# First attention layer by key/value group, its value and score products in high and low parts, four heads side by side

## The chip, the cores and the metric

The kernel runs on one core of one Trainium2 chip. A core has a tensor engine for matrix products (PE, with its weight loads shown apart as PEld), VectorE (DVE), ScalarE (ACT), GpSimd (POOL) and SyncE (SP), which here only issues transfers. Each engine works through its own list of instructions in order; semaphores join the lists. SBUF is the working memory, PSUM holds the results of products in eight banks of 512 fp32 columns. The metric is the device time of one launch in microseconds (us), lower is better.

## The reference, cut to what matters

Four layers follow each other, each with an attention part and a feed-forward part that read the same normalized input and are added to the stream `x` of 2 x 1024 tokens of width 256. Only the first layer's attention is touched. It has 16 query heads of width 128 in 4 groups; the 4 heads of a group share one key head and one value head. (The lines below leave out a multiplication and division by a layer index of 1; the drawn shapes are those that the kernel runs, 2 batches of 1024 tokens.)

```python
xn = _layernorm(x, axis=-1)
q = jnp.einsum('bsh,he->bse', x, w_q).reshape(b, sq, GROUPS, HPG, KVC)
kv = jnp.einsum('bsh,he->bse', x, w_kv)
k, v = jnp.split(kv, 2, axis=-1)
...
scores = jnp.einsum('bqgpd,bkgd->bgqpk', q, k) * (SCALE / LAYER_INDEX)
...
scores = jnp.where(causal[None, None, :, None, :], scores, -jnp.inf)
probs = jax.nn.softmax(scores, axis=-1).astype(x.dtype)
ctx = jnp.einsum('bgqpk,bkgd->bqgpd', probs, v).reshape(b, sq, HEADS * KVC)
return jnp.einsum('bse,eh->bsh', ctx, w_dense)
```

## The kernel before

Everything is kept turned, features on the 128 partitions and tokens along the free side. `XT` is the stream, `XN` the normalized stream, and `XH`, `XL` are `XN` split in two: a high part rounded to the type float32r and the low part that the rounding left. `split_product` (line 199) makes one precise product of three float32r ones (high with high, high with low, low with high), for each of the two halves of the width of 256; the projections use it. The other products of this attention (scores, values, dense) are plain fp32; the profile records two instructions for one of these.

`l0_attn` calls two stages. `l0_kv` loads the whole key/value weight, splits it, and projects all keys `KT` and values `V` in 32 jobs of 512 columns over eight banks. `l0_heads` then loops over the 16 heads. Its unit u is one tile of 128 queries: U = 16 units a head, 8 in each batch, and tile t of a batch sees t+1 blocks of 128 keys. One head is a software pipeline, written out in its order in each engine's loop body, over steps s:

- PE: `scores(s)` into one of two score banks of 1024 columns (line 355), then `turn_probs(s-2)`, which transposes the blocks of probabilities (369), `dense(s-4)` (391), and `weigh_values(s-3)` with 128 columns at a time (382). The queries of the next head are projected in the last steps, into the score banks.
- DVE: `invert(s-1)` (459), `row_max(s)` with causal mask, maximum and its negative (450 to 454), `keep_turned(s-2)` for every second group of up to four turned blocks (470), `add_dense(s-4)` into `XT` (475).
- ACT: `keep_ctxT(s-4)` (521), `keep_turned(s-2)` for the other groups (514), `exp(s)` with its row sum (528), and the copies of the queries (497).
- POOL multiplies the probabilities by the inverse of the sum (424) and makes the low part of the query weight (413).

SP loads each head's query and dense weights ahead of their use. What holds a score bank is the chain of scores, mask, maximum, negative, exp; four buffers of probabilities follow it. The wait of ACT's turned copy is only for PE:

```python
act.wait_ge(turned, h * G + n + 1)
if u >= 2:
    act.wait_ge(pv_done, h * U + u - 1)
```

Of the kernel before, what the change touches and what calls it, by code (L numbers as in the profile page):

```python
# [16 lines left out]
P = 128  # L17
# [191 lines left out]
def l0_attn(nc, k, a):  # L209
    with Stage(nc, "l0a") as st:  # L210
        KT = st.sb("KT", [P, L0_GROUPS, T])
        V = st.sb("V", [P, TT, L0_GROUPS * L0_HD])
        l0_kv(nc, k, a, KT, V)
        l0_heads(nc, k, a, KT, V)


def l0_kv(nc, k, a, KT, V):

    with Stage(nc, "l0kv") as st:
        acc = [st.ps(f"acc{i}") for i in range(8)]  # L220
        w_loaded, made, kept_act, kept_dve = st.sem("w_loaded"), st.sem("made"), st.sem("kept_act"), st.sem("kept_dve")
        GD = L0_GROUPS * L0_HD
        wkv = st.sb("wkv", [P, DC, 2 * GD])
        w_hi, w_lo = st.sb("w_hi", [P, DC, 2 * GD], F32R), st.sb("w_lo", [P, DC, 2 * GD], F32R)
        whi_ready, wlo_ready = st.sem("whi_ready"), st.sem("wlo_ready")

        jobs = [("k", g, j) for g in range(L0_GROUPS) for j in range(NJ)] + [("v", t, 0) for t in range(TT)]

        def target(n):
            kind, i, j = jobs[n]  # L230
            return KT[:, i, j * BANK:(j + 1) * BANK] if kind == "k" else V[:, i, :]

        with nc.Block() as block:

            @block.sync
            def _(sp):
                sp.dma_start(wkv[:, :, :], rows(a["L0_attn_w_kv"])).then_inc(w_loaded, 16)

            @block.tensor
            def _(pe):  # L240
                pe.wait_ge(wlo_ready, DC)
                for n, (kind, i, j) in enumerate(jobs):
                    if n >= 8:
                        pe.wait_ge(kept_act if n % 2 == 0 else kept_dve, (n - 8) // 2 + 1)
                    if kind == "k":
                        tok, col = slice(j * BANK, (j + 1) * BANK), slice(i * P, (i + 1) * P)
                        mm = split_product(pe, acc[n % 8][:, :], lambda c: w_hi[:, c, col], lambda c: w_lo[:, c, col],
                                           lambda c: k.XH[:, c, tok], lambda c: k.XL[:, c, tok])
                    else:
                        tok, col = slice(i * P, (i + 1) * P), slice(GD, 2 * GD)  # L250
                        mm = split_product(pe, acc[n % 8][:, :], lambda c: k.XH[:, c, tok], lambda c: k.XL[:, c, tok],
                                           lambda c: w_hi[:, c, col], lambda c: w_lo[:, c, col])
                    mm.then_inc(made, 1)

            @block.scalar
            def _(act):
                act.wait_ge(w_loaded, 16)
                for c in range(DC):
                    act.activation(w_hi[:, c, :], wkv[:, c, :], ACT.Copy).then_inc(whi_ready, 1)
                for n in range(0, len(jobs), 2):  # L260
                    act.wait_ge(made, n + 1)
                    act.activation(target(n), acc[n % 8][:, :], ACT.Copy).then_inc(kept_act, 1)

            @block.vector
            def _(dve):
                for c in range(DC):
                    dve.wait_ge(whi_ready, c + 1)
                    dve.tensor_tensor(w_lo[:, c, :], wkv[:, c, :], w_hi[:, c, :].bitcast(F32), ALU.subtract).then_inc(wlo_ready, 1)
                for n in range(1, len(jobs), 2):
                    dve.wait_ge(made, n + 1)  # L270
                    dve.tensor_copy(target(n), acc[n % 8][:, :]).then_inc(kept_dve, 1)


def l0_heads(nc, k, a, KT, V):


    U = B * NQ
    GPB = sum(-(-(t + 1) // 4) for t in range(NQ))
    G = B * GPB
    group_of = [(u, g) for u in range(U) for g in range(-(-(u % NQ + 1) // 4))]  # L280
    first_group = [group_of.index((u, 0)) for u in range(U)]

    with Stage(nc, "l0h") as st:
        wq = st.sb("wq", [P, DC, P])
        wq_hi, wq_lo = st.sb("wq_hi", [P, DC, P], F32R), st.sb("wq_lo", [P, DC, P], F32R)
        whi_ready, wlo_ready = st.sem("whi_ready"), st.sem("wlo_ready")
        wd = st.sb("wd", [P, D])
        QT = st.sb("QT", [P, T])
        probs = st.sb("probs", [P, 4, S])
        VG = st.sb("VG", [P, TT, P])  # L290
        PT = st.sb("PT", [P, 2, NQ, P])
        ctxT = st.sb("ctxT", [P, 2, P])
        top = st.sb("top", [P, 2])
        negtop = st.sb("negtop", [P, 2])
        total = st.sb("total", [P, 4])
        inv = st.sb("inv", [P, 4])
        sc = [st.ps(f"sc{i}", 2 * BANK) for i in range(2)]
        tp = [st.ps(f"tp{i}") for i in range(2)]
        cx = st.ps("cx")
        outp = st.ps("outp")  # L300
# [2478 lines left out]
```

## Time and profile before

| | |
|---|---|
| median of 3 runs | 3993.09 us (3988.18 to 3993.31) |
| the profiled execution's own time | 3988.51 us |
| its span, first to last instruction | 3986.7 us |
| mean granted clock of PE over the span | 0.932 |
| busy share of the span | PE 89%, PEld 66%, DVE 59%, ACT 39%, POOL 35% |

A share over the whole span mixes four layers. The changed stages are the first quarter of the span, and what they are bound by is read there. "Idle before" in a group of instructions is the time in which its engine stood before them, with what ended it. A record of a product includes the tail in which the array empties, which overlaps the next product; the distance between starts is what a product takes in a row of them.

### The profile page before, as it was taken

How to read it: one execution, taken by the hardware profiler on the slowest of the kernel's cores; microseconds unless marked ns; L12 is line 12 of the kernel's file. 1: busy time of each engine (PE TensorE's matmuls, PEld its weight loads, DVE VectorE, ACT ScalarE, POOL GpSimd, SP SyncE). 2: the span in 40 equal slices, each digit the busy share in tenths (PEclk: the TensorE clock that was granted, in tenths of full speed). 3: DMA queues.
4: the chain of work that ended last, by engine and by line, in shares of the span. 5: the costliest groups of instructions: out<-in, count | busy, mean ns of one | idle time of the engine just before them, and what ended most of it. 6: DMA issues, size and time to landing. Idle time of an engine off the chain costs nothing. (4 is left out here: it accounts for less than half of the span.)

```text
span 3986.7 us, 65977 instructions
## 1 busy us (share of the span) xinstructions
PE 3548.5 (89%) x21608; PEld 2615.5 (66%) x21608; DVE 2353.9 (59%) x4783; ACT 1557.1 (39%) x2820; POOL 1383.1 (35%) x1085
## 2 busy tenths in 40 slices
PE   6899999999797999999986599999699997999576
PEld 4777777777575888888862344444388856886354
DVE  3555555655423656666655677775477746776444
ACT  2444444444333444444432246664233333333111
POOL 1333333333133666666643200000133352335144
PEclk8999999999898999999998889999799998999755
DMA  0000000000001000000002311221233303331144
GB/s 33 7 5 3 5 5 5 3 5 5 32 0 43 18 18 17 17 17 17 17 0 74 121 74 75 76 75 40 64 93 105 98 15 101 93 104 49 58 107 96
DMA packets 115990, 178.66 MB, mean 45 GB/s; under 512 B 22288, under 2 KB 65040, under 8 KB 115600
## 3 DMA queue, kind: packets, MB, share of 16 engines
q1 hardware_dynamic: 109776, 169.38, 13.8%
q0 software_dynamic: 6144, 8.39, 1.3%
q8 instruction: 38, 0.62, 0.1%
q14 instruction: 32, 0.26, 0.0%
HBM read 151.51 MB, written 25.95 MB: 45 GB/s over the span
## 5 line engine op out<-in xcount | busy, mean ns | idle before, releaser
L424 POOL TENSOR_TENSOR l0h_probs<-l0h_probs,l0h_inv 128x128 f32<-128x128 f32 (+7 forms) x256 | 292.8, 1146 | 585.7 <-DVE l0h_inv L459 585.7
L1747 DVE TENSOR_REDUCE l2h_half<-l2h_s 128x1 f32<-128x512 f32 x512 | 329.5, 685 | 94.9 <-PE l2h_s L1658 94.9
L1734 ACT ACTIVATE l2h_PT<-l2h_s 128x1024 f32<-128x1024 f32 x256 | 261.9, 1023 | 194.9 <-PE l2h_s L1668 194.6
L355 PE MATMUL l0h_sc<-l0a_KT,l0h_QT 128*128 x768 | 296.8, 499 | 30.0 <-ACT l0h_probs L528 28.4
L382 PE MATMUL l0h_cx<-l0h_PT,l0h_VG 128*128 128x128 f32 x2304 | 300.7, 276 | 0.0
L528 ACT ACTIVATE l0h_probs<-l0h_sc,l0h_negtop 128x128 f32<-128x128 f32 (+7 forms) x256 | 189.7, 741 | 245.3 <-DVE l0h_negtop L454 244.9
L382 PEld LDWEIGHTS l0h_cx<-l0h_PT,l0h_VG 128*128 128x128 f32 x2304 | 278.0, 192 | 1.0
L159 POOL TENSOR_TENSOR XN<-XN,n_rstd 128x512 f32<-128x512 f32 x32 | 39.9, 1266 | 633.6 <-DVE n_rstd L140 633.6
L1658 PE MATMUL l2h_s<-l2h_K,l2h_Q 128*128 128x512 f32 x512 | 180.1, 428 | 22.5 <-DMA l2h_K<-l_split 18.8
L452 DVE TENSOR_REDUCE l0h_top<-l0h_sc 128x1 f32<-128x128 f32 (+7 forms) x256 | 194.0, 758 | 8.8
L355 PEld LDWEIGHTS l0h_sc<-l0a_KT,l0h_QT 128*128 128x128 f32 x768 | 125.6, 192 | 106.6 <-issue 63.7
L1668 PE MATMUL l2h_s<-l2h_Q,l2h_K 128*128 128x512 f32 x512 | 187.2, 447 | 1.0 <-DMA l2h_Q<-l2h_mlo 0.6
L391 PE MATMUL l0h_outp<-l0h_ctxT,l0h_wd 128*128 128x128 f32 x1024 | 163.8, 283 | 24.9 <-ACT l0h_ctxT L521 11.7
L369 PEld LDWEIGHTS l0h_tp<-ident,l0h_probs 128*128 128x128 f32 x1152 | 138.5, 141 | 64.2 <-issue 39.6
L369 PE MATMUL l0h_tp<-ident,l0h_probs 128*128 128x128 f32 x1152 | 168.7, 274 | 0.0
L470 DVE COPY l0h_PT<-l0h_tp 128x256 f32<-128x256 f32 (+2 forms) x192 | 98.6, 514 | 114.2 <-PE l0h_tp L369 112.3
L2158 POOL TENSOR_TENSOR l3p_w_lo<-l3p_w,l3p_w_hi 128x1024 fp32r<-128x1024 f32 x34 | 80.1, 2356 | 241.4 <-ACT l3p_w_hi L2114 241.4
L391 PEld LDWEIGHTS l0h_outp<-l0h_ctxT,l0h_wd 128*128 128x128 f32 x1024 | 134.2, 191 | 44.7 <-ACT l0h_ctxT L521 31.2
L514 ACT ACTIVATE l0h_PT<-l0h_tp 128x512 f32<-128x512 f32 (+1 forms) x192 | 100.8, 525 | 159.7 <-PE l0h_tp L369 159.2
L2190 DVE TENSOR_TENSOR_SCAN l3p_table<-l3p_decb,l3p_eye 128x512 f32<-128x512 f32 x128 | 149.6, 1210 | 23.0 <-DMA l3p_blk<-c_l_block 17.4
L1680 PE MATMUL l2h_pv<-l2h_PT,l2h_VH 128*32 128x256 f32 x2048 | 162.1, 391 | 0.2 <-ACT l2h_ctxT L1725 0.2
L2148 POOL TENSOR_TENSOR l3a_Y<-l3p_skip,l3p_sz 128x512 f32 (+1 forms) x64 | 81.7, 1276 | 209.3 <-DVE l3p_skip L2181 209.3
(408 smaller groups left out, 8869.8 us busy)
## 6 DMA issues: line engine op xcount, KB each, us to landing
l3p_decb<-l_decays SPq DMA_DIRECT2D x128, 256.0 KB, 4.2
l3p_w<-L_w SPq DMA_DIRECT2D x34, 512.0 KB, 3.7
l2h_Q<-l_split SPq DMA_DIRECT2D x64, 256.0 KB
l2h_K<-l_split SPq DMA_DIRECT2D x64, 256.0 KB
l3p_prow<-l_decays SPq DMA_DIRECT2D x128, 128.0 KB, 3.0
l_split<-l2q_hi SPq DMA_DIRECT2D x16, 512.0 KB, 3.8
l_split<-l2q_lo SPq DMA_DIRECT2D x16, 512.0 KB, 3.8
mx_wgu<-L_ffn_w_gate_up SPq DMA_DIRECT2D x32, 256.0 KB
```

The source lines that it names most:

```text
L355: mm = pe.matmul(sc[u % 2][:, lo:lo + n], QT[:, u * P:(u + 1) * P], KT[:, ds(g, 1), b * S + lo:b * S + lo + n], start=True, stop=True)
L369: mm = pe.transpose(tp[n % 2][:, (kb - q) * P:(kb - q + 1) * P], probs[:, u % 4, kb * P:(kb + 1) * P], k.ident[:, :])
L382: mm = pe.matmul(cx[:, 0:P], VG[:, b * NQ + kb, :], PT[:, u % 2, kb, :], start=(kb == 0), stop=(kb == t))
L391: mm = pe.matmul(outp[:, c * P:(c + 1) * P], wd[:, c * P:(c + 1) * P], ctxT[:, u % 2, :], start=True, stop=True)
L424: pool.tensor_tensor(p, p, inv[:, u % 4:u % 4 + 1].to_broadcast([P, keys(u)]), ALU.mult).then_inc(probs_scaled, 1)
L452: dve.reduce_max(top[:, u % 2:u % 2 + 1], sc[u % 2][:, 0:keys(u)], AX_X).then_inc(top_ready, 1)
L528: act.activation(probs[:, u % 4, 0:keys(u)], sc[u % 2][:, 0:keys(u)], ACT.Exp, bias=negtop[:, u % 2:u % 2 + 1], scale=L0_SCALE, accum_out= ...
L1658: pe.matmul(s1[i % 2][:, :], Q1[:, b, t * P:(t + 1) * P], K1[:, b, z * BANK:(z + 1) * BANK], start=True, stop=True).then_inc(s1_made, 1)
L1668: mm = pe.matmul(s2[kb % 2][:, z * BANK:(z + 1) * BANK], K2[:, b, kb * P:(kb + 1) * P], Q2[:, b, z * BANK:(z + 1) * BANK], start=True, sto ...
L1680: mm = pe.matmul(pv[g * L2_W:(g + 1) * L2_W, 0:2 * P], VH[:, b, kb, :], PT[:, b, kb, g * 2 * P:(g + 1) * 2 * P], start=(kb == 0), stop=(kb ...
L1734: act.activation(PT[:, b, kb, :], s2[kb % 2][:, :], ACT.Exp, scale=L2_SCALE).then_inc(exped, 1)
L1747: dve.reduce_max(half[:, b, t, z:z + 1], s1[i % 2][:, :], AX_X).then_inc(maxed, 1)
```

## The change

`l0_attn` becomes one stage. The outer order is key/value group, then batch, then query tile: 64 units u, and inside each unit the 4 heads of the group. A "cell" is a group and batch, 8 units.

- Values: the four heads' turned probabilities of one key block lie side by side in one bank, 512 columns. ACT rounds them to a high part `PTH`, DVE subtracts it to make the low part `PTL`, and PE makes three float32r products for each block (values high with `PTH`, values low with `PTH`, values high with `PTL`) in place of four fp32 ones of 128 columns.
- Scores: queries and keys are kept in high and low parts (`QH`, `QL`, `KH`, `KL`), three float32r products for each piece of up to 512 keys.
- Dense: the context is kept in parts as well (`CH`, `CL`), and one float32r product handles two tiles (256 columns) of one head; it is made and added for each second unit.
- Projections are made between the units (`extra`): k of a cell as 12 products of 512 columns, v as 48 of 128, and q for two tiles and four heads as 24 of 256. Each is kept by one ACT copy of 1024 columns and one DVE subtraction of 1024 columns.
- Scores, projections and dense take turns on two pools of two banks (`bank(item)`); an item may start when the item before the last has been read. Three banks hold turned blocks, one the context.
- Probabilities have two buffers of four heads, the first of them in `XN`. The loops are written out in full; SP loads weights by group in three kinds.

The core of the diff (PE's project functions, the weight splits and POOL's scaling, which is as before for each unit and head, are left out):

```diff
+                def scores(u, h):
...
+                    for lo in range(0, (t + 1) * P, BANK):
+                        key = slice(lo, min(lo + BANK, (t + 1) * P))
+                        out = bank(item)[:, key]
+                        pe.matmul(out, QH[:, p % 2, h, q], KH[:, b, key], start=True, stop=False)
+                        pe.matmul(out, QH[:, p % 2, h, q], KL[:, b, key], start=False, stop=False)
+                        mm = pe.matmul(out, QL[:, p % 2, h, q], KH[:, b, key], start=False, stop=True)
+                    mm.then_inc(scores_made, 1)
+                def turn(u, kb):
+                    n = blocks_ahead[u] + kb
+                    wait(pe, pt_low, n - 2)
+                    for h in range(HG):
+                        if kb == 0:
+                            pe.wait_ge(probs_scaled, HG * u + h + 1)
+                        mm = pe.transpose(tp[n % 3][:, h * P:(h + 1) * P], probs[u % 2][:, h, kb * P:(kb + 1) * P], k.ident[:, :])
+                    mm.then_inc(turned, 1)
+                def values(u, kb):
...
+                    pe.wait_ge(pt_high, n + 1)
+                    pe.matmul(cx[:, :], VH[:, b, kb, :], PTH[:, n % 3, :], start=(kb == 0), stop=False)
+                    pe.matmul(cx[:, :], VL[:, b, kb, :], PTH[:, n % 3, :], start=False, stop=False)
+                    pe.wait_ge(pt_low, n + 1)
+                    pe.matmul(cx[:, :], VH[:, b, kb, :], PTL[:, n % 3, :], start=False, stop=(kb == t)).then_inc(values_made, 1)
...
+                            for h in range(HG):
+                                pe.matmul(out, wd_hi[:, h, col], CH[:, h, :, :], start=(h == 0), stop=False)
+                                pe.matmul(out, wd_hi[:, h, col], CL[:, h, :, :], start=False, stop=False)
+                                mm = pe.matmul(out, wd_lo[:, h, col], CH[:, h, :, :], start=False, stop=(h == HG - 1))
...
+                for u in range(UNITS + 2):
+                    scores(u, 0)
+                    last_values(u - 2)
+                    if u < UNITS:
+                        project_extra(extra(u))
+                    scores(u, 1)
+                    turn_and_weigh(u - 1, 0)
+                    scores(u, 2)
+                    turn_and_weigh(u - 1, 1)
+                    dense(u - 2)
+                    scores(u, 3)
+                    turn_and_weigh(u - 1, 2)
+                    turn_and_weigh(u - 1, 3)
...
+                            act.wait_ge(turned, n + 1)
+                            wait(act, values_made, n - 2)
+                            act.activation(PTH[:, n % 3, :], tp[n % 3][:, :], ACT.Copy).then_inc(pt_high, 1)
...
+                    exp(u, 0)
+                    keep_context(u - 2)
+                    if u < UNITS:
+                        keep_high(extra(u))
+                    exp(u, 1)
+                    keep_turned(u - 1, 0)
+                    exp(u, 2)
+                    keep_turned(u - 1, 1)
+                    exp(u, 3)
+                    keep_turned(u - 1, 2)
+                    keep_turned(u - 1, 3)
...
+                            dve.wait_ge(pt_high, n + 1)
+                            dve.tensor_tensor(PTL[:, n % 3, :], tp[n % 3][:, :], PTH[:, n % 3, :].bitcast(F32), ALU.subtract).then_inc(pt_low, 1)
...
+                for u in range(UNITS + 2):
+                    row_max(u, 0)
+                    keep_context(u - 2)
+                    if u < UNITS:
+                        keep_low(extra(u))
+                    row_max(u, 1)
+                    invert(u, 0)
+                    keep_turned(u - 1, 0)
+                    row_max(u, 2)
+                    invert(u, 1)
+                    keep_turned(u - 1, 1)
+                    add_dense(u - 2)
+                    row_max(u, 3)
+                    invert(u, 2)
+                    keep_turned(u - 1, 2)
+                    invert(u, 3)
+                    keep_turned(u - 1, 3)
```

`keep_turned(u, part)` and `turn_and_weigh(u, part)` handle a quarter of the unit's t+1 key blocks. PE turns block kb and then weighs block kb-2; `last_values` weighs the last two, a unit later. q is projected at tiles 0, 2 and 4, and the next cell's k, v and first q at tiles 5, 6 and 7.

## Rows read from the trace of the kernel before

**Rows 1.** The page: busy us, share of the span, instructions.
```profile
PE 3548.5 (89%) x21608; PEld 2615.5 (66%) x21608; DVE 2353.9 (59%) x4783; ACT 1557.1 (39%) x2820; POOL 1383.1 (35%) x1085
```

**Rows 2.** Timeline, where the changed code begins and ends: start us, us, engine line op.
```profile
45.59 0.38 SPq L237 DMA_DIRECT2D l0kv_wkv<-L_attn_w_kv  x1
...
1044.01 0.42 DVE L475 TENSOR_TENSOR XT<-XT,l0h_outp 128x256 f32<-128x256 f32 x1 [2.44 <-PE l0h_outp L391]
```

**Rows 3.** Windows: window, length, each engine's busy time (instructions), granted clock, DMA share, GB/s.
```profile
45.60:112.70 67.10, 54.00 (x216) 43.97 (x217) 13.43 (x18) 13.78 (x22) 2.69 (x3) 0.85 0.07 22
112.70:1044.50 931.80, 876.36 (x5633) 701.00 (x5631) 527.63 (x1472) 419.26 (x1057) 309.75 (x278) 1.00 0.01 4
1250.00:1300.00 50.00, 27.42 (x158) 22.51 (x157) 20.05 (x33) 20.11 (x32) 26.56 (x22) 0.73 0.25 85
2220.00:2320.00 100.00, 61.47 (x225) 36.93 (x226) 61.72 (x65) 11.15 (x17) 11.92 (x7) 0.69 0.16 59
```

**Rows 4.** Groups by line, PE: shapes xcount, busy us, mean ns, idle before and releasers.
```profile
L382 PE MATMUL l0h_cx<-l0h_PT,l0h_VG 128*128 128x128 f32 x2304 | 300.7, 276 | 0.0
L355 PE MATMUL l0h_sc<-l0a_KT,l0h_QT 128*128 x768 | 296.8, 499 | 30.0 <-ACT l0h_probs L528 28.4 <-issue 1.2 <-ACT l0h_QT L497 0.5
```

**Rows 5.** Timeline of PE, five places: projections at both clock levels, and a head.
```profile
55.19 0.63 PE L199 MATMUL l0kv_acc<-x_XH,l0kv_w_lo 128*128 128x512 f32 x1
55.61 0.63 PE L199 MATMUL l0kv_acc<-x_XH,l0kv_w_hi 128*128 128x512 f32 x1
...
60.08 0.39 PE L199 MATMUL l0kv_acc<-x_XL,l0kv_w_hi 128*128 128x512 f32 x1
60.31 0.40 PE L199 MATMUL l0kv_acc<-x_XH,l0kv_w_lo 128*128 128x512 f32 x1
...
485.04 1.04 PE L369 MATMUL l0h_tp<-ident,l0h_probs 128*128 128x128 f32 x8
485.91 0.61 PE L391 MATMUL l0h_outp<-l0h_ctxT,l0h_wd 128*128 128x128 f32 x4
486.36 1.73 PE L382 MATMUL l0h_cx<-l0h_PT,l0h_VG 128*128 128x128 f32 x14
487.92 0.81 PE L355 MATMUL l0h_sc<-l0a_KT,l0h_QT 128*128 x2
488.57 0.27 PE L369 MATMUL l0h_tp<-ident,l0h_probs 128*128 128x128 f32 x1
...
505.38 0.47 PE L199 MATMUL l0h_sc<-x_XH,l0h_wq_hi 128*128 128x512 f32 x1
505.70 0.39 PE L199 MATMUL l0h_sc<-x_XL,l0h_wq_hi 128*128 128x512 f32 x1
```

**Rows 6.** Groups by line and form, DVE and ACT; of the reduce and exp the longest and shortest of eight.
```profile
L452 DVE TENSOR_REDUCE l0h_top<-l0h_sc 128x1 f32<-128x1024 f32 x32 | 39.2, 1225 | 1.1
...
L452 DVE TENSOR_REDUCE l0h_top<-l0h_sc 128x1 f32<-128x128 f32 x32 | 9.3, 292 | 1.1
...
L268 DVE TENSOR_TENSOR l0kv_w_lo<-l0kv_wkv,l0kv_w_hi 128x1024 fp32r<-128x1024 f32 x2 | 2.4, 1221 | 6.4 <-ACT l0kv_w_hi L259 6.4
...
L528 ACT ACTIVATE l0h_probs<-l0h_sc,l0h_negtop 128x1024 f32<-128x1024 f32 x32 | 35.8, 1117 | 26.5 <-DVE l0h_negtop L454 26.5
...
L528 ACT ACTIVATE l0h_probs<-l0h_sc,l0h_negtop 128x128 f32<-128x128 f32 x32 | 11.8, 367 | 18.8 <-DVE l0h_negtop L454 18.8
...
L514 ACT ACTIVATE l0h_PT<-l0h_tp 128x512 f32<-128x512 f32 x128 | 76.4, 597 | 151.1 <-PE l0h_tp L369 151.1
```

**Rows 7.** Timeline of DVE and ACT: a 512 column copy and its successor, a row_max and its exp.
```profile
498.27 0.69 DVE L470 COPY l0h_PT<-l0h_tp 128x512 f32<-128x512 f32 x1
498.88 0.41 DVE L475 TENSOR_TENSOR XT<-XT,l0h_outp 128x256 f32<-128x256 f32 x1
...
503.45 0.30 DVE L450 TENSOR_TENSOR l0h_sc<-l0h_sc,causal 128x128 f32<-128x128 f32 x1 [0.66 <-PE l0h_sc L355]
503.78 1.22 DVE L452 TENSOR_REDUCE l0h_top<-l0h_sc 128x1 f32<-128x1024 f32 x1
...
505.31 1.12 ACT L528 ACTIVATE l0h_probs<-l0h_sc,l0h_negtop 128x1024 f32<-128x1024 f32 x1 [0.82 <-DVE l0h_negtop L454]
```

More of the change, by code:

```diff
@@ L209, in l0_attn @@
 def l0_attn(nc, k, a):
-    with Stage(nc, "l0a") as st:
[L211 to L231, printed above, removed]
+    UNITS = L0_GROUPS * B * NQ
@@ new lines, in l0_attn, with place, extra @@
+    HG = L0_HPG
+    PAIR = 2 * P
+    blocks_ahead = [0]
+    for u in range(UNITS):
+        blocks_ahead.append(blocks_ahead[-1] + u % NQ + 1)
+    def place(u):
+        return u // (B * NQ), u // NQ % B, u % NQ
+    def extra(u):
+        g, b, t = place(u)
+        cell = u // NQ
+        if t in (0, 2, 4):
+            return ("q", cell, t // 2 + 1)
+        if t >= 5 and cell + 1 < B * L0_GROUPS:
+            return {5: ("k", cell + 1), 6: ("v", cell + 1), 7: ("q", cell + 1, 0)}[t]
+        return None
@@ new lines, in l0_attn, with quarter @@
+    number = {}
+    for item in (("k", 0), ("v", 0), ("q", 0, 0)):
+        number[item] = len(number)
+    for u in range(UNITS + 2):
+        order = [("s", u, 0), extra(u) if u < UNITS else None, ("s", u, 1), ("s", u, 2), ("d", u // 2 - 1) if u >= 2 and u % 2 else None, ("s", u, 3)]
+        for item in order:
+            if item is not None and (item[0] != "s" or u < UNITS):
+                number[item] = len(number)
+    def quarter(u, part):
+        n = u % NQ + 1
+        return range(part * n // 4, (part + 1) * n // 4)
@@ L255, in _, with split_wkv @@
             @block.scalar
             def _(act):
[L257 to L262, printed above, removed]
+                def split_wkv(g):
+                    act.wait_ge(wkv_loaded, 32 * g + 32)
+                    wait(act, v_made, B * g)
+                    act.activation(wkv_hi[:, :, :, :], wkv[:, :, :, :], ACT.Copy).then_inc(wkv_high, 1)
@@ new lines, in exp @@
+                def exp(u, h):
+                    if u >= UNITS:
+                        return
+                    item, n = ("s", u, h), HG * u + h
+                    keys = (u % NQ + 1) * P
+                    act.wait_ge(negtop_ready, n + 1)
+                    if u >= 2:
+                        act.wait_ge(turned, blocks_ahead[u - 1])
+                    act.activation(probs[u % 2][:, h, 0:keys], bank(item)[:, 0:keys], ACT.Exp, bias=negtop[:, h:h + 1], scale=L0_SCALE,
+                                   accum_out=total[:, n % (2 * HG):n % (2 * HG) + 1]).then_inc(read(item), 1)
@@ new lines, in keep_turned, with keep_context @@
+                def keep_turned(u, part):
+                    if 0 <= u < UNITS:
+                        for kb in quarter(u, part):
+                            n = blocks_ahead[u] + kb
+                            act.wait_ge(turned, n + 1)
+                            wait(act, values_made, n - 2)
+                            act.activation(PTH[:, n % 3, :], tp[n % 3][:, :], ACT.Copy).then_inc(pt_high, 1)
+                def keep_context(u):
+                    if 0 <= u < UNITS:
+                        act.wait_ge(values_made, blocks_ahead[u + 1])
+                        wait(act, dense_made, u // 2)
+                        act.activation(CH[:, :, u % 2, :], cx[:, :].rearrange("p (h n) -> p h n", h=HG), ACT.Copy).then_inc(ctx_high, 1)
@@ new lines, in add_dense @@
+                def add_dense(u):
+                    if u >= 0 and u % 2:
+                        item = ("d", u // 2)
+                        g, b, t = place(u)
+                        tok = b * S + t // 2 * PAIR
+                        dve.wait_ge(dense_made, u // 2 + 1)
+                        x = k.XT[:, :, tok:tok + PAIR]
+                        dve.tensor_tensor(x, x, bank(item)[:, 0:DC * PAIR].rearrange("p (c n) -> p c n", c=DC), ALU.add).then_inc(read(item), 1)
+                for item in (("k", 0), ("v", 0), ("q", 0, 0)):
+                    keep_low(item)
```

476 lines of the change are left out of this document (226 added, 250 removed).

## The prediction, made before the changed kernel was run

> **What bounds the kernel now.** I read the page's busy line first: PE is busy 89% of the span [rows 1]. The timeline brackets the changed code: SyncE issues the old key/value load at 45.6 us, the last addition of the attention ends at 1044.4 [rows 2], 998.8 us. The windows split that: 67.1 us until the first scores, then 931.8 us in which PE is busy 876.4, VectorE (DVE) 527.6 and ScalarE (ACT) 419.3, at the full clock [rows 3]. The groups by line say what PE is short of: its scores stood 30.0 us, nearly all until exp gave back a score bank [rows 4]. So before, PE sets the time and the others follow. The question is whether that stays so.
>
> **PE's work, before and after.** Distances between starts in the PE timeline give prices: a high/low (fp32r) product of 512 columns 0.23 us; a plain fp32 record of 128 columns 0.111, two records for one product; scores in fp32 0.65 for 384 columns, 0.215 for each 128; a transpose 0.109 [rows 5]. Before: 2,304 value records [rows 4] 257 us, scores (147,456 columns) 248, 1,152 transposes 125, 1,024 dense records 114, 600 products of projections 137: 881 us. After: 864 value products at 0.228 make 197, k's 96 make 22. No row shows fp32r under 512 columns. For 128 columns the ends are a quarter of the 512 price, 0.057, and the whole fp32 product, 0.223; I take 0.112, the price of an fp32 record, nearest because it too brings 128 columns of weights. For 256 the ends are 0.114 and 0.43 (two fp32 pieces of scores); I take 0.12, for 384 0.17. Then the scores, three products for one, cost 209, 768 q products 92, 768 dense products 92, 384 v products 43, transposes 125. The first fp32r product behind fp32 ones takes 0.32 instead of 0.23 [rows 5]; 288 such changes, 26. Sum 806 us, 75 less than before.
>
> The Trainium skill (TensorE: Matmul & The Clock Gate, "LDWEIGHTS (loading the stationary operand)") puts a weight load at its columns divided by 1.2 GHz, an estimate of 107 ns for 128 columns. No row here shows a load-bound fp32r product; 384 v products would be 41 us by it, against my 43.
>
> **DVE and ACT, and the order between them.** DVE's new work is low parts: 288 of turned probabilities and 64 of context (0.69 us recorded, the next begins after 0.61 [rows 7]), 48 of 1,024 columns (1.22 [rows 6]). With row_max and invert as before its sum is some 617 us (327, 176, 39, 55, dense 20); ACT's some 510. Both are under PE's. But they don't run beside each other. Take unit u (one group, batch and tile t; t = 0..7 has (t+1)x128 keys; 64 units in 8 "cells" of eight). DVE's order is row_max(u,h+1), invert, keep_turned(u-1,..), row_max(u,h+2); ACT's is exp(u,h+1), keep_turned(u-1,..), exp(u,h+2). DVE's keep_turned waits for pt_high, which ACT makes only behind exp(u,h+1), and that waits for the row_max that DVE has just done. Behind DVE's waiting subtraction stands the next row_max, and for that waits the next exp. The two take turns. Before, DVE's and ACT's copies were of separate blocks, neither needed the other's.
>
> The price of one turn. From mask to exp's start it is 0.635 us plus the reduce (503.45 to 505.31 with a reduce of 1.22) [rows 7]. Over eight lengths the reduce runs from 0.292 to 1.225 and exp from 0.367 to 1.117, in nearly even steps [rows 6]. So row_max plus exp is S = 1.29, 1.53, 1.77, 2.01, 2.25, 2.49, 2.73, 2.98 us for t = 0..7. A step with n turned blocks costs S + 0.65 (ACT's high copy, 0.60 [rows 6], and a handover) + 0.61n + 0.09 for invert; one without blocks only the reduce + 0.52. The first head's step holds keep_context, S + 0.60 + 0.61, and where a projection comes, 1.6 more (its high copy beside the context's low one, then the low one). Unit t turns the t blocks of the unit before (8 at t=0), in four quarters. At t=7: 5.8 + 4.3 + 4.95 + 0.6 (add_dense) + 6.1 = 21.7 us. All, t = 0..7: 15.0, 8.0, 11.8, 12.3, 16.4, 18.6, 19.5, 21.7, a cell 123.3, in all 986. PE by the prices above (a block 1.2: 0.43 transposes, 0.68 values, 0.09 change): 13.8, 6.2, 6.5, 9.1, 11.6, 15.6, 17.2, 19.5, a cell 99.5. The turns are longer in every unit.
>
> The Trainium skill (TensorE: Matmul & The Clock Gate, "Architectural detail: the array is 16× 32×32, not 1× 128×128") calls the queues of ACT and DVE strictly first in, first out. The trace agrees in that mask, reduce and exp come in program order [rows 7]; if the next row_max could pass the waiting copy, the sum would be PE's, case D below.
>
> **What PE adds to the turns.** Scores, projections and dense share two banks. A projection runs behind scores(u,0) and last_values, and its copies stand in the chain. t=0: 0.3 + 1.4 + 2.9 (24 q products) end at 4.7, so its low part ends at 6.7 instead of 4.1; the last blocks wait 0.8 for values ahead of their transposes: +3.4. t=1: dense (24 products, 2.9) needs exp(u,1), and behind it stand add_dense and the last row_max: +2.8. In the same way t=3 +0.8, t=4 +0.9, t=5 +1.3, t=7 +2.6. t=6: v is 48 products, 5.4 us, low part at 10.0 instead of 5.5: +4.5. Together 16.3 a cell, 130 us.
>
> **The sum.** 986 + 130 = 1,116; the first cell has no earlier blocks (-8), the last no next projections (-12): 1,096. Lead-in 23 us from 45.6: load, wkv's high part on ACT and low part on POOL 5, k at the 0.427 us that products cost at 1.2 GHz [rows 5] 5, v 6, q 4, q's copies 3; the splits of wq and wd hide behind k and v. It replaces the 67.1, in which the separate pass of keys and values was [rows 3]. Drain 17: eight blocks without exp, a context, dense, the addition. Total 1,136 against 998.8: +137. At no price: POOL's scaling stays and its 12 splits lie in its idle time (busy 309.8 of 931.8 [rows 3]); uncovered, 2.4 us each. SP's 15 later loads are issued when the splits have read the buffer, a group ahead; uncovered, some 3 us each. The clock: stretches of this kernel with PE busy at 55% and 61% had 0.73 and 0.69 granted, at 94% 1.00 [rows 3]; here PE would be busy 72%. For a mean a little under full on the PE pieces in the chain (35 us a cell) I add 15, with ends 0 and 60. So +152: 3988.5, the profiled execution's own time (span 3986.7 and 1.8 around it), becomes 4140.5. It lies 4.6 under the median of the runs, so 4145.
>
> **Rivals.** A, the forecast, DVE and ACT in turns: chance 0.58, 4055 to 4185.
> B, short fp32r products cost what fp32 does. B1, only those of 128 columns, 0.223: 48 in each t=6 chain, +43 us, 4190: 0.14. B2, those of 256 too, 0.43: q and dense add 476 us to PE, which then binds, with v and scores some 4450: 0.05. Nothing in the trace excludes either.
> C, 0.12: PE falls to 1.2 GHz for long parts. At a mean of 0.7, as in rows 3, its 35 us a cell become 50, +120 for +15; PE's other work half hides: 4190 to 4240.
> D, 0.08, the other sign: handovers cost less than the steps I add up, and PE stays the bound. 806 + lead-in and drain 40 + 98 of idle (nearly twice the 55 of before) are 944, 55 less than before: 3938. For it speaks that no sum but PE's exceeds 620 us, against it the order of the two queues. It decides where each of some 224 steps is 0.6 us shorter than I price it, as long as the whole high copy: then the 137 are gone.
> E, 0.03: the turns hold but hide all of PE: 986 - 20 + 40 = 1,006, about 4000, no measurable change.
>
> **How the numbers follow.** A run of this kernel tells 0.2%, 8 us, from no change. A, B and C are slower, 0.89; E 0.03 is the same, D 0.08 faster. The range leaves D, E and B2 out, 0.16: from 4055, where half of PE's 130 is hidden and the clock full, to 4235.
>
> **What would show it.** The first scores near 69 us; cells of eight units some 140 us long; DVE and ACT busy about 58% and 47% of the stretch and seldom together; DVE's low parts of turned blocks with idle before them that ends on ACT's high copy; exp's idle ending on negtop; PE busy near 72%. Starts of 256- and 128-column fp32r products 0.12 and 0.112 apart. The forecast is wrong if DVE starts a row_max while ACT still makes the high copy before it, if a cell is near 110 us, or if 256-column products start 0.4 us apart.

## The result, and the profile after

| | before | after |
|---|---|---|
| median | 3992.14 us (3988.18 to 3993.31, 4 runs) | 4108.66 us (4100.89 to 4110.28, 4 runs) |
| span of the profiled execution | 3986.7 us | 4106.9 us |
| mean granted clock | 0.932 | 0.92 |

The changed kernel is slower: ratio 1.029, 95% interval 1.0272 to 1.0308, 116.5 us. The forecast was 4145 us, 152 more than before; the time lies in its range, 4055 to 4235. (Medians of the kernel before differ by chip, from 3985 to 3998 us. So every experiment stands with its ratio to runs of before on its own chip.)

The page of after, busy us and share of the span. Beside [rows 1], PE does less and DVE more, and neither share tells where 120 us of span come from:

```profile
PE 3534.4 (86%) x20944; PEld 2621.4 (64%) x20944; DVE 2433.4 (59%) x4749; ACT 1573.5 (38%) x2666; POOL 1390.9 (34%) x1072
```

The timeline of after at the start of the changed stage, at its first mask and at its last addition, as in [rows 2]:

```profile
44.15 0.89 SPq L286 DMA_DIRECT2D l0a_wkv<-L_attn_w_kv  x2
...
65.12 0.30 DVE L548 TENSOR_TENSOR l0a_sc<-l0a_sc,causal 128x128 f32<-128x128 f32 x1 [0.64 <-PE l0a_sc L358]
...
1152.63 0.69 DVE L600 TENSOR_TENSOR XT<-XT,l0a_sc 128x512 f32<-128x512 f32 x1 [3.24 <-PE l0a_sc L407]
```

The stage takes from 44.15 to 1153.3, which is 1109.2 us in place of 998.8: +110.4. The other 9.8 of the 120.2 fall outside the stage.

The windows of after, with columns as there: the body of the stage, then two pieces of it. [Rows 3] had PE busy 94% at a clock of 1.00, here it is 82% at 0.96. No engine is full:

```profile
65.00:1019.00 954.00, 783.98 (x4500) 642.75 (x4500) 539.51 (x1273) 387.27 (x805) 275.58 (x234) 0.96 0.01 4
...
210.00:350.00 140.00, 113.79 (x657) 93.48 (x656) 80.04 (x191) 57.15 (x121) 39.91 (x35) 0.96 0.01 4
...
630.00:770.00 140.00, 114.46 (x678) 93.00 (x676) 80.03 (x188) 57.65 (x120) 40.39 (x34) 0.99 0.02 5
```

The waits of after in the stage: who waited for whom, us in total, times, longest. They form the ring of the forecast: ACT's exp for DVE's negative maximum, DVE's low part for ACT's high part:

```profile
ACT l0a_probs L467 <- DVE l0a_negtop L552: 302.7, 128, 6.3
ACT XN L467 <- DVE l0a_negtop L552: 253.4, 128, 3.2
DVE l0a_PTL L585 <- ACT l0a_PTH L476: 210.8, 181, 1.7
...
PE l0a_cx L378 <- ACT l0a_PTH L476: 91.2, 88, 2.2
```

The last row is a second leg, which the forecast had not priced: PE's value products wait for the same high copy, and the scores that follow in PE's order stand behind them.

One unit with eight blocks, first DVE, then ACT. In square brackets is the idle time before:

```profile
311.84 0.29 DVE L548 TENSOR_TENSOR l0a_sc<-l0a_sc,causal 128x128 f32<-128x128 f32 x1
312.16 1.22 DVE L550 TENSOR_REDUCE l0a_top<-l0a_sc 128x1 f32<-128x1024 f32 x1
313.42 0.15 DVE L552 TENSOR_SCALAR l0a_negtop<-l0a_top 128x1 f32<-128x1 f32 x1
313.49 0.15 DVE L559 RECIPROCAL l0a_inv<-l0a_total 128x1 f32<-128x1 f32 x1
315.33 0.69 DVE L585 TENSOR_TENSOR l0a_PTL<-l0a_tp,l0a_PTH 128x512 fp32r<-128x512 f32 x1 [1.69 <-ACT l0a_PTH L476]
315.94 0.29 DVE L548 TENSOR_TENSOR l0a_sc<-l0a_sc,causal 128x128 f32<-128x128 f32 x1
```

```profile
313.61 1.11 ACT L467 ACTIVATE l0a_probs<-l0a_sc,l0a_negtop 128x1024 f32<-128x1024 f32 x1 [2.94 <-DVE l0a_negtop L552]
314.62 0.19 ACT L467 ACTIVATION_READ_ACCUMULATOR l0a_probs<-l0a_sc,l0a_negtop 128x1 f32 x1
314.71 0.59 ACT L476 ACTIVATE l0a_PTH<-l0a_tp 128x512 fp32r<-128x512 f32 x1
317.71 1.12 ACT L467 ACTIVATE l0a_probs<-l0a_sc,l0a_negtop 128x1024 f32<-128x1024 f32 x1 [2.41 <-DVE l0a_negtop L552]
```

Follow one turn: mask at 311.84, exp at 313.61, high copy at 314.71, low copy at 315.33, next mask at 315.94. It takes 4.10 us, in which ACT stands 2.41 and DVE 1.69; in this turn neither works on a long instruction while the other does.

### The profile page after: what moved, and what is told of

Read it like the earlier page. It is cut to its first block and busy times, and to the rows that moved or that the text cites. A ratio compares the mean times of both kernels' runs of the same rounds, so it can differ in the third digit from the quotient of the medians.

```text
span 4106.9 us, 61659 instructions
## 1 busy us (share of the span) xinstructions
PE 3534.4 (86%) x20944; PEld 2621.4 (64%) x20944; DVE 2433.4 (59%) x4749; ACT 1573.5 (38%) x2666; POOL 1390.9 (34%) x1072
## 5 line engine op out<-in xcount | busy, mean ns | idle before, releaser
L1811 ACT ACTIVATE l2h_PT<-l2h_s 128x1024 f32<-128x1024 f32 x256 | 262.1, 1024 | 194.6 <-PE l2h_s L1745 194.5
L585 DVE TENSOR_TENSOR l0a_PTL<-l0a_tp,l0a_PTH 128x512 fp32r<-128x512 f32 x288 | 191.8, 686 | 210.8 <-ACT l0a_PTH L476 210.8
L538 POOL TENSOR_TENSOR l0a_probs<-l0a_probs,l0a_inv 128x256 f32<-128x256 f32 (+3 forms) x128 | 160.6, 1255 | 364.7 <-DVE l0a_inv L559 362.7
L538 POOL TENSOR_TENSOR XN<-XN,l0a_inv 128x128 f32<-128x128 f32 (+3 forms) x128 | 133.3, 1041 | 403.5 <-DVE l0a_inv L559 403.5
L467 ACT ACTIVATE l0a_probs<-l0a_sc,l0a_negtop 128x256 f32<-128x256 f32 (+3 forms) x128 | 101.8, 795 | 302.7 <-DVE l0a_negtop L552 302.7
L378 PE MATMUL l0a_cx<-l0a_PTH,l0a_VH 128*128 128x512 f32 x288 | 134.2, 466 | 91.8 <-ACT l0a_PTH L476 91.2
L356 PE MATMUL l0a_sc<-l0a_KH,l0a_QH 128*128 128x512 f32 (+3 forms) x384 | 147.7, 385 | 67.0 <-DVE l0a_QL L568 38.9
L550 DVE TENSOR_REDUCE l0a_top<-l0a_sc 128x1 f32<-128x128 f32 (+7 forms) x256 | 194.0, 758 | 8.7
L467 ACT ACTIVATE XN<-l0a_sc,l0a_negtop 128x128 f32<-128x128 f32 (+3 forms) x128 | 88.1, 688 | 253.4 <-DVE l0a_negtop L552 253.4
L476 ACT ACTIVATE l0a_PTH<-l0a_tp 128x512 fp32r<-128x512 f32 x288 | 159.2, 594 | 15.8 <-PE l0a_tp L367 15.8
L1735 PEld LDWEIGHTS l2h_s<-l2h_K,l2h_Q 128*128 128x128 f32 x512 | 99.3, 194 | 79.5 <-DVE l2h_half L1824 31.5
```

The source lines that it names most:

```text
L356: pe.matmul(out, QH[:, p % 2, h, q], KH[:, b, key], start=True, stop=False)
L467: act.activation(probs[u % 2][:, h, 0:keys], bank(item)[:, 0:keys], ACT.Exp, bias=negtop[:, h:h + 1], scale=L0_SCALE, accum_out=total[:, n ...
L476: act.activation(PTH[:, n % 3, :], tp[n % 3][:, :], ACT.Copy).then_inc(pt_high, 1)
L538: pool.tensor_tensor(p, p, inv[:, n % (2 * HG):n % (2 * HG) + 1].to_broadcast([P, (t + 1) * P]), ALU.mult).then_inc(probs_scaled, 1)
L550: dve.reduce_max(top[:, h:h + 1], bank(item)[:, 0:(t + 1) * P], AX_X).then_inc(top_ready, 1)
L585: dve.tensor_tensor(PTL[:, n % 3, :], tp[n % 3][:, :], PTH[:, n % 3, :].bitcast(F32), ALU.subtract).then_inc(pt_low, 1)
```

## The experiments

A cell is counted from the first head's mask of its t=0 to that of the next cell. The column has the second to the seventh cell; the first is 9 to 18 us shorter in every kernel, its first units having few earlier blocks or none. "One run" marks a kernel that ran once; its time has no interval.

| run | time, us | ratio to before, interval | cell, us |
|---|---|---|---|
| after | 4108.66 | 1.029, 1.0272 to 1.0308 | 136.4 (136.0 to 137.9) |
| e1 copy before exp | 3978.67 | 0.9956, 0.9939 to 0.9972 | 119 to 122 |
| e1c, the same again | 3972.49 | 0.9963, 0.9949 to 0.9976 | 119 to 122 |
| e2 fewer products | 4179.87, one run | | 147 |
| e3 second high copy | 4219.87, one run | | 149 to 154 |
| e4 short v | 4085.92 | 1.0222, 1.0205 to 1.0239 | 133 to 137 |
| e5b project later | 3981.58 | 0.9989, 0.998 to 0.9999 | 119 to 123 |
| e6b dense later | 4011.94 | 1.0062, 1.0045 to 1.0079 | 123 to 126 |
| e7b padded products | 4143.49, one run | | 143 |
| e8b plain values | 4033.14 | 1.0114, 1.0097 to 1.0131 | 127 to 130 |
| e9 plain values, copy before exp | 3991.67 | 1.0015, 1.0006 to 1.0024 | 122 to 125 |

**Is it the order?** e1 changes ACT's order alone: each quarter of turned blocks is copied ahead of the exp that it stood behind.

```diff
-                    exp(u, 1)
                     keep_turned(u - 1, 0)
-                    exp(u, 2)
+                    exp(u, 1)
                     keep_turned(u - 1, 1)
-                    exp(u, 3)
+                    exp(u, 2)
                     keep_turned(u - 1, 2)
+                    exp(u, 3)
                     keep_turned(u - 1, 3)
```

> ScalarE's order only: each quarter's high copies of turned probabilities (keep_turned) stand ahead of the exp of the next head, not behind it. Every instruction, wait and product is kept. Theory (DVE and ACT take turns): the high copy is then made while DVE does the row_max, and exp while DVE subtracts; a step of a head loses exp and the high copy from the chain, about 0.65 to 1.7 us each, until PE's 13.8 to 19.5 us a unit bind: cells of about 116 us instead of 136, the whole near 3960 us, which is less than the kernel before. Rival, PE is the bound already: no change, 4108. Rival, the two score banks bind: cells stay above 130, about 4060 to 4100.

3978.67 us: 130 less than after, with the same work; expected was near 3960. DVE's low copies, in the groups by line of e1 (busy us, mean ns, idle before), stood 30.3 us before them in place of 210.8, and PE's wait for the high copy fell from 91.2 to 10.4:

```profile
L585 DVE TENSOR_TENSOR l0a_PTL<-l0a_tp,l0a_PTH 128x512 fp32r<-128x512 f32 x288 | 191.3, 681 | 30.3 <-ACT l0a_PTH L476 29.0
```

The kernel was measured again, since it also beats the kernel before:

> The same kernel as e1, again, on the chip of e9 and in more rounds: is it faster than the kernel before by more than 0.2%? The first time 0.9956 of before. If that holds 3970 to 3985; if it was the chip, a ratio of 1.000.

0.9963: it holds. The same kind of unit in the timelines of e1c, DVE and then ACT:

```profile
285.31 0.29 DVE L548 TENSOR_TENSOR l0a_sc<-l0a_sc,causal 128x128 f32<-128x128 f32 x1
285.64 1.23 DVE L550 TENSOR_REDUCE l0a_top<-l0a_sc 128x1 f32<-128x1024 f32 x1
...
287.04 0.67 DVE L585 TENSOR_TENSOR l0a_PTL<-l0a_tp,l0a_PTH 128x512 fp32r<-128x512 f32 x1
287.62 0.29 DVE L548 TENSOR_TENSOR l0a_sc<-l0a_sc,causal 128x128 f32<-128x128 f32 x1
287.95 1.23 DVE L550 TENSOR_REDUCE l0a_top<-l0a_sc 128x1 f32<-128x1024 f32 x1
```

```profile
284.94 0.60 ACT L476 ACTIVATE l0a_PTH<-l0a_tp 128x512 fp32r<-128x512 f32 x1 [0.80 <-PE l0a_tp L367]
287.08 1.12 ACT L467 ACTIVATE l0a_probs<-l0a_sc,l0a_negtop 128x1024 f32<-128x1024 f32 x1 [1.55 <-DVE l0a_negtop L552]
...
288.19 1.08 ACT L476 ACTIVATE l0a_PTH<-l0a_tp 128x512 fp32r<-128x512 f32 x2
289.40 1.12 ACT L467 ACTIVATE l0a_probs<-l0a_sc,l0a_negtop 128x1024 f32<-128x1024 f32 x1
```

ACT's next two high copies, from 288.19 to 289.27, run beside DVE's reduce of 287.95, and DVE's low copy of 287.04 beside the exp of 287.08. (The first high copy, at 284.94, was over just before its reduce began.) From mask to mask are 2.31 us, not 4.10.

**Does ACT's time lie on the path in full?** e3 gives ACT one more copy of 512 columns before each high copy.

```diff
+                            act.activation(spare[:, n % 3, :], tp[n % 3][:, :], ACT.Copy)
                             act.activation(PTH[:, n % 3, :], tp[n % 3][:, :], ACT.Copy).then_inc(pt_high, 1)
```

> Adds to each of the 288 high copies of turned probabilities one more ACT copy of the same 512 columns into a buffer that nobody reads, ahead of it. ACT's busy time rises by some 155 us, from 450 of a 1,109 us stretch, so ACT has the idle time for it three times over. Theory (turns): each block's high copy comes 0.54 us later and DVE waits for it, +18 us a cell, 4108 becomes about 4250. Rival, PE or DVE's own sum is the bound: under +20 us.

111 us more than after, by 13.9 us in most cells: the theory held, at less than its 18 a cell, and the rival of under 20 us did not. In ACT's timeline of e3 the added copy is recorded at 0.59 us, but the next one starts 0.48 after it:

```profile
396.80 0.59 ACT L477 ACTIVATE l0a_spare<-l0a_tp 128x512 f32<-128x512 f32 x1
397.28 0.60 ACT L478 ACTIVATE l0a_PTH<-l0a_tp 128x512 fp32r<-128x512 f32 x1
```

288 times 0.48 are 138 us, so four fifths of the added time reached the end, although ACT was busy only half of the time. The row is the windows' of e3:

```profile
210.00:350.00 140.00, 106.38 (x591) 85.35 (x589) 72.72 (x170) 67.61 (x141) 37.08 (x32) 0.95 0.01 4
```

**Does PE's v projection lie on the path?** e4 makes v of 16 products, high with high, in place of 48.

```diff
-                        mm = split_product(pe, bank(item)[:, n * P:(n + 1) * P], lambda c: k.XH[:, c, tok], lambda c: k.XL[:, c, tok],
-                                           lambda c: wkv_hi[:, c, 1, :], lambda c: wkv_lo[:, c, 1, :])
+                        for c in range(DC):
+                            mm = pe.matmul(bank(item)[:, n * P:(n + 1) * P], k.XH[:, c, tok], wkv_hi[:, c, 1, :], start=(c == 0), stop=(c == DC - 1))
```

> Leaves out two of the three products of each piece of the value projection (16 products of 128 columns for each cell and not 48, high with high only). PE loses 32 x 0.111 = 3.6 us in each of eight cells. Theory (the projection of v stands in the chain of the unit at tile 6, before its copies): seven of the eight are paid in full, -25 us for them, and the one of the lead-in with some 3 more: about 4080 us, the unit at tile 6 goes from 23.2 to 19.6 us. Rival, PE's pieces are hidden behind DVE and ACT: no change beyond the noise.

The t=6 unit fell from 23.2 to 19.6 us in most cells; 32 products at 0.111 are 3.6. The other units stayed there. By the two ratios the kernel is 0.7% shorter than after, 27 us, where 28 were expected.

**Is PE's amount of work the bound?** e2 makes one product of each three in scores and values.

```diff
-                        pe.matmul(out, QH[:, p % 2, h, q], KH[:, b, key], start=True, stop=False)
-                        pe.matmul(out, QH[:, p % 2, h, q], KL[:, b, key], start=False, stop=False)
-                        mm = pe.matmul(out, QL[:, p % 2, h, q], KH[:, b, key], start=False, stop=True)
+                        mm = pe.matmul(out, QH[:, p % 2, h, q], KH[:, b, key], start=True, stop=True)
...
-                    pe.matmul(cx[:, :], VH[:, b, kb, :], PTH[:, n % 3, :], start=(kb == 0), stop=False)
-                    pe.matmul(cx[:, :], VL[:, b, kb, :], PTH[:, n % 3, :], start=False, stop=False)
                     pe.wait_ge(pt_low, n + 1)
-                    pe.matmul(cx[:, :], VH[:, b, kb, :], PTL[:, n % 3, :], start=False, stop=(kb == t)).then_inc(values_made, 1)
+                    pe.matmul(cx[:, :], VH[:, b, kb, :], PTH[:, n % 3, :], start=(kb == 0), stop=(kb == t)).then_inc(values_made, 1)
```

> Leaves out two of the three products of each score piece and of each value block (only high with high is computed, so the low parts of queries, keys, values and probabilities don't enter there); all copies, waits and the order are kept. PE loses about 270 us of products. Theory (turns of DVE and ACT): only the pieces of PE that stand in the chain get shorter (the first scores and last values ahead of each projection), some 7 us a cell, so about 4050 us. Rival, PE is the bound: about 3840 us. Rival, a lower clock of PE costs much: the granted clock falls further and the time hardly falls.

The expectation had the wrong sign: the kernel takes 71 us more than after. The windows of e2 point at the cause, a granted clock of 0.77 in place of 0.96:

```profile
210.00:350.00 140.00, 92.73 (x452) 77.05 (x453) 75.48 (x177) 53.84 (x112) 38.66 (x33) 0.77 0.01 4
```

PE's timeline of e2 holds both levels in one dense projection, behind a wait of 2.37 us. Starts are 0.213 apart until 373.68, at 1.2 GHz, and 0.12 from 373.86, at 2.4:

```profile
370.77 0.55 PE L401 MATMUL l0a_sc<-l0a_CH,l0a_wd_hi 128*128 128x256 f32 x1 [2.37 <-ACT l0a_probs L463]
...
373.04 0.41 PE L402 MATMUL l0a_sc<-l0a_CL,l0a_wd_hi 128*128 128x256 f32 x1
373.25 0.41 PE L403 MATMUL l0a_sc<-l0a_CH,l0a_wd_lo 128*128 128x256 f32 x1
...
373.98 0.28 PE L401 MATMUL l0a_sc<-l0a_CH,l0a_wd_hi 128*128 128x256 f32 x1
374.10 0.28 PE L402 MATMUL l0a_sc<-l0a_CL,l0a_wd_hi 128*128 128x256 f32 x1
```

The masks say where the time went. Of the 10.4 us that a cell grew, 9.0 are in three steps from the first mask of a unit to the second, those that hold the projections of q, k and v: at t=0 from 6.24 to 8.35 us, at t=5 from 5.65 to 8.23, at t=6 from 8.90 to 13.18. The steps without PE's projections or dense products kept their length within 0.2 us, but for t=0's last one, 0.3 shorter.

To test that cause, e7b keeps e2's short products and puts two products of 512 columns ahead of each group of transposes, some 131 us of PE work whose results are overwritten.

```diff
+                    for z in range(2):
+                        pe.matmul(tp[n % 3][:, :], k.XH[:, 0, 0:P], k.XH[:, 0, 0:BANK], start=True, stop=True)
                     for h in range(HG):
```

> The kernel with fewer products (two of three products of scores and values left out) with two extra products of 512 columns ahead of each of the 288 groups of transposes, written to the bank that the transposes then overwrite, read by nobody. PE gets 131 us of work more. Theory (the 4180 us with fewer products came from the granted clock, 0.75 in that stretch against 0.95): the clock rises to 0.85 or more, the fixed pieces of PE in the chain get shorter, and the time falls below that kernel's although there is more to do: 4080 to 4140 us. Rival, it was slow for its longer wait for the low part or another order of waits: the time stays at 4180 or rises by up to 100.

4143.49 us, less than e2 with more to do, and the clock of the windows rose:

```profile
210.00:350.00 140.00, 100.60 (x542) 83.05 (x542) 74.92 (x178) 54.31 (x114) 38.62 (x32) 0.88 0.01 4
```

The next stage began at 1202.10 us, e2's at 1229.27. So the amount of work that e2 left out was not what bound after, and thinning it out cost clock. That the added products also moved other waits is not excluded by this run alone. The Trainium skill (TensorE: Matmul & The Clock Gate, "Part 1: The HAM clock gate (the "warmup" mystery)") says "the default state is throttled, and activity releases the throttle"; these two runs agree with that.

**What holds e1 at 119 us a cell?** Four runs bear on it. e5b is e1 with the projection behind the second head's scores, and its copies behind the second exp and row_max. (The lines show PE's part. The order of the banks follows, and ACT's high copies of the first quarter of turned blocks are back behind the second exp, as in after.)

```diff
                     last_values(u - 2)
+                    scores(u, 1)
                     if u < UNITS:
                         project_extra(extra(u))
-                    scores(u, 1)
```

> On top of the first experiment (high copies ahead of exp), the projection of a unit comes after scores(u,1) on PE, and in the order of the banks; its high and low copies come after exp(u,1) and row_max(u,1). All work is kept. Theory: in the first experiment's kernel the units at tiles 0, 2 and 4 still wait for PE's 2.9 us and the two copies before the second head's row_max; that goes behind the row_max and exp now, 1 to 2 us for each of the five units with a projection, cells from 119 to about 113, near 3935 us. Rival, these units are bound by PE's own sum: no change, 3978.

No gain: cells as in e1, the time that the rival named. The masks tell why, and it isn't PE's sum: the first step of a unit got shorter and the second longer by as much. At t=6 they were 8.90 + 2.18 us in e1 and are 3.87 + 7.40 now; the projection was moved, not hidden. e6b moves dense behind the last head's scores too, and its addition behind the third quarter's low copies.

```diff
-                    dense(u - 2)
                     scores(u, 3)
+                    dense(u - 2)
```

> The kernel with the later projection, and with the dense product of a pair of tiles after scores(u,3), and its addition after the row_max and the copies of that head. All work is kept. Theory: at tiles 1 and 3 PE's 2.9 us of dense and the addition stand ahead of the last head's scores and row_max, though DVE has little else to do there; moved behind, those units fall from 12.2 and 13 us to 10 or 11, cells to about 109, near 3910 us. Rival, the next unit's scores wait for the dense bank in its place: no change against the kernel with the later projection alone.

Neither theory nor rival held: e6b is slower than e5b by 0.7%. The waits of e6b, as above:

```profile
ACT l0a_PTH L476 <- PE l0a_tp L367: 184.2, 117, 5.3
...
PE l0a_sc L356 <- ACT l0a_probs L467: 42.6, 41, 2.0
```

In e5b they were 113.7 and 9.2. Scores now wait for exp to give back their bank, and the dense products stand straight ahead of the transposes that ACT's copy needs. At t=7 the third step fell from 4.93 to 2.91 us, and the fourth rose from 5.06 to 8.42.

e8b is after, not e1, with values in plain fp32: V and the turned probabilities are kept whole, DVE's low copies of both are gone, and PE makes one fp32 product of 512 columns for each block. The core of the edit:

```diff
-                    pe.matmul(cx[:, :], VH[:, b, kb, :], PTH[:, n % 3, :], start=(kb == 0), stop=False)
-                    pe.matmul(cx[:, :], VL[:, b, kb, :], PTH[:, n % 3, :], start=False, stop=False)
-                    pe.wait_ge(pt_low, n + 1)
-                    pe.matmul(cx[:, :], VH[:, b, kb, :], PTL[:, n % 3, :], start=False, stop=(kb == t)).then_inc(values_made, 1)
+                    pe.matmul(cx[:, :], VH[:, b, kb, :], PTH[:, n % 3, :], start=(kb == 0), stop=(kb == t)).then_inc(values_made, 1)
```

> The changed kernel with one part undone: the value products are plain fp32, one product of 512 columns for each key block from an unsplit V and unsplit turned probabilities. ACT still copies all 288 turned blocks, in its old place behind exp; DVE makes no low parts of them or of V. The order of everything else is kept. PE's products of a block go from 0.68 to about 0.86 us, +51 us of PE in all. Theory (turns): DVE has no copy that waits for ACT, so the turns are broken although PE has more to do: cells of 110 to 116 us, 3920 to 3960 us, less than both kernels. Rival, PE is the bound: about +30 to +50 us, 4150. Rival, the two banks bind: 4050 to 4100.

75 us less than after, about half of the least that was expected, and outside what both rivals named. Removing the handover to DVE altogether, with some 51 us more for PE, gave less than e1's order did. In its waits the largest of DVE's is now that for scores, 15.4 us in after:

```profile
DVE l0a_sc L545 <- PE l0a_sc L358: 210.3, 105, 4.7
```

The second leg is left: PE's values still waited 38.1 us for ACT's copy behind exp. e9 takes both cures, e8b with e1's order on ACT.

> The two cures at once: ACT's copy of the turned probabilities ahead of exp, as in e1, and plain fp32 values without DVE's low parts, as in e8. Values are exact in fp32, nothing is left out. In e1 a cell took 119 us, in e8 129, in the kernel after 136. Theory 1, the handover from ACT's high copy to DVE's low copy is still what binds e1: without it a cell falls to 108 to 112 us and the time to some 3900 (7 cells of 9 less than e1). Theory 2, once ACT's copy no longer waits behind exp, PE's own order of scores, transposes and values over the two pools binds: the low copies cost nothing more, the plain values cost PE 0.86 against 0.77 us a block (288 blocks, 26 us), a cell stays at 119 to 123 and the time at 3980 to 4005. I hold theory 2 for likelier, since PE was busy 122 to 126 us of 140 in e1.

3991.67 us, 0.5% above e1c on the same chip, as its second theory had it. The windows of e1 and of e9 over the same stretch: DVE's 614 us became 430, and the end did not come sooner, while PE did a little more.

```profile
65.00:1019.00 954.00, 842.81 (x5072) 729.04 (x5073) 613.76 (x1452) 447.36 (x918) 310.37 (x265) 0.96 0.01 4
```

```profile
65.00:1019.00 954.00, 855.20 (x4682) 660.43 (x4682) 429.94 (x1148) 437.02 (x898) 301.95 (x262) 0.96 0.01 4
```

The four cells together: low copies and the old order 136.4, plain values and the old order 129, low copies and the new order 119 to 122, plain values and the new order 122 to 125. Under the old order the low copies cost 7 us a cell, under the new one they gain some 3, which is about the 0.09 us for each of 36 blocks that PE saves by them. And without any low copy the order is still worth 6: that part is the leg between ACT and PE. One handover of the same kind is left in e1 and was not tried: DVE stands 89.4 us there before the 64 low parts of the context, for ACT's high part, which comes behind the first head's exp.

## Why the prediction was right, and where it was off

**The mechanism.** Case A, DVE and ACT in turns. Shown by e1: the same instructions in another order on ACT alone give back all of the loss and a little more. e8b and e9 add that the ring had two legs, of which the forecast named DVE's; ACT's copy behind exp held PE up as well. e3 and e4 show the two kinds of term, ACT's copies and PE's v, each on the path.

**The sum.** 1,136 us were forecast for the stage, 1109.2 measured. Unit by unit, t = 0..7, in us:

| | 0 | 1 | 2 | 3 | 4 | 5 | 6 | 7 | cell |
|---|---|---|---|---|---|---|---|---|---|
| forecast, turns and PE's part | 18.4 | 10.8 | 11.8 | 13.1 | 17.3 | 19.9 | 24.0 | 24.3 | 139.6 |
| measured | 17.4 | 12.3 | 12.6 | 13.0 | 16.6 | 19.0 | 23.2 | 22.3 | 136.4 |
| shortest of each step | 17.1 | 10.8 | 12.6 | 13.0 | 16.6 | 19.0 | 23.2 | 22.3 | 134.4 |

The second row is the cell as it comes four times, second to fifth, within 0.1 us. The last takes each step from mask to mask where it was shortest in the second to seventh cell, so that, as the next paragraph shows, it holds next to nothing of the low clock. (The cell is summed before rounding.) Set against it, the sum of turns and PE's part was 5 us a cell too high. Of the miss of 27 in the stage the six full cells are some 18, the first 5, the lead-in 2 (21.0, not 23), the last cell and the drain 2.

The mis-sized terms are two. One is the price of a turn. At t=7 a step with one block was put at 2.98 + 0.65 + 0.61 + 0.09 = 4.33 and took 4.10: row_max plus exp were 1.77 + 1.10 = 2.87, and invert ran while ACT made exp, at no price. At t=0, 2, 4, 5 and 6 steps with one or two blocks were 0.22 or 0.23 shorter than priced as well. The other is what PE adds at t=0 and t=7, put at 3.4 and 2.6 us; each came out some 1 to 1.5 us smaller, an estimate from the same masks. At t=7 PE makes its dense products inside a step of 5.30 us (its third, of 315.94), for which the turn alone had been priced 4.95 + 0.6, so they added nothing. One term was too low: at t=2 the forecast let PE add nothing, and the first step, with a q projection, took 5.74 us instead of the 4.6 priced.

**The clock.** The forecast added 15 us for it, and the trace of after bears the size out. The cells repeat each other step by step, but the short stretches at 1.2 GHz do not fall alike in all of them. From the third mask of t=1 to the fourth, with 24 dense products between, it took 6.00 us in the second to fifth cell and 4.51 in the sixth and seventh. PE's timeline, third cell and then seventh, has starts 0.21 apart in the one, 1.2 GHz, and 0.12 in the other, 2.4:

```profile
350.96 0.41 PE L405 MATMUL l0a_sc<-l0a_CH,l0a_wd_hi 128*128 128x256 f32 x1
351.17 0.41 PE L406 MATMUL l0a_sc<-l0a_CL,l0a_wd_hi 128*128 128x256 f32 x1
...
895.34 0.28 PE L405 MATMUL l0a_sc<-l0a_CH,l0a_wd_hi 128*128 128x256 f32 x1
895.46 0.28 PE L406 MATMUL l0a_sc<-l0a_CL,l0a_wd_hi 128*128 128x256 f32 x1
```

In the sixth and seventh cell the dense of t=3 was met instead, 6.30 us against 4.81. What the steps took beyond the shortest of their kind is 2.0 us in each of the second to fifth cells and 17.5 us up to the end of the seventh; this is an estimate of the clock's cost, from the masks. Without it the stage would take some 1092 us, 44 less than the 1,136 of the sum. So the turns and PE's part were 44 too high and the clock's 15 was 2 or 3 too low, which makes the 42 by which 152 exceeds 110.4.

The 9.8 us outside the stage, for which nothing was forecast, brought the forecast 10 us nearer (152 against 120.2 of span). That is luck: they can't be shown to be an effect of the change. All the changed kernels run the same code behind the stage as before does, and from the stage's last addition to the end it took 2939.6 to 2953.5 us in their traces and 2942.3 in before's.

**The prices of short products.** PE's timeline of after has both, so B1 and B2 fall. 128 columns, starts 0.11 apart:

```profile
53.83 0.28 PE L199 MATMUL l0a_sc<-l0a_wkv_lo,x_XH 128*128 128x128 f32 x1
53.94 0.28 PE L199 MATMUL l0a_sc<-l0a_wkv_hi,x_XL 128*128 128x128 f32 x1
54.05 0.28 PE L199 MATMUL l0a_sc<-l0a_wkv_hi,x_XH 128*128 128x128 f32 x1
...
59.36 0.28 PE L199 MATMUL l0a_sc<-x_XH,l0a_wq_lo 128*128 128x256 f32 x1
59.48 0.28 PE L199 MATMUL l0a_sc<-x_XH,l0a_wq_hi 128*128 128x256 f32 x1
```

The last two are of 256 columns, 0.12 apart. The estimate of 107 ns that the prediction took from the Trainium skill (TensorE: Matmul & The Clock Gate, "LDWEIGHTS (loading the stationary operand)") lies 4 ns under the 0.111 of 128 columns; that the load is what sets this distance, no run here shows.

**The signs named.** First mask at 65.1 us, just ahead of the 69 named; cells 136; DVE's low parts with idle before them ended by ACT's high copy; exp's idle ended by negtop: all seen. DVE was busy 57% of the body (58 forecast), ACT 41%, not 47: its sum of 510 us, given without its parts, was 448 in the stage. PE was busy 82%, not 72: the forecast divided a sum of distances between starts by the time, and records hold the tails too, so the sign was put in the wrong measure.

**The other rivals.** C, a clock at 0.7, did not come in this kernel, with 0.96; in e2, with PE's products thinned, it was 0.77. D, PE as the bound, would have made the kernel faster than before. Even e1, with the turns broken, reaches a cell of 119 us against the 99.5 of PE's summed work, and 3975, not 3938. E falls with the time itself and with e4, since PE's parts were not hidden. What keeps e1 some 20 us a cell above PE's sum is not settled. Moving projections or dense does not win it, removing DVE's low copies does not, the wait for the context's high part (89.4 us, 11 a cell) was not tried, and PE is busy 843 of 954 us there.

## What to carry to other kernels

Where two engines share a datum within one step, write each one's order down beside the other's and look for a ring: here each had 40 to 60% of its time free, and together they set the end. The cure here was to put the producer's copy ahead of the instruction that waits for the consumer's other work; that order was worth 3.2% of the kernel, and it made the change a gain of 0.4% instead of a loss of 2.9%. Where the units of a kernel repeat, set the same step of several of them side by side: what a low clock costs can be read off without an experiment. Price short steps from start to start of the profile's rows, and leave out small instructions that run while the partner works.

## What was not expected of the hardware

Taking products away from PE, 92.7 us busy of 140 in place of 113.8, made the kernel 71 us slower, and the next stage began 75 us later (one run): the granted clock fell from 0.96 to 0.77, and 256 column products took 0.213 us in place of 0.12 for long parts. Added products without use brought 0.88, and the next stage began 27 us sooner than in e2 (one run of each). Where long pieces of PE, here the projections, stand in the chain that sets the time, thinner work on PE is no safe gain.
